# Hidden rows of four groups in one bank, an unrolled edge stage, and the pair adds dealt out anew

## The reference, cut to what matters

```python
s = hs[idx_j]; v = hv[idx_j]                 # rows of the edge's far node, 32 and 32 x 3
ys = Yr_ij[:, 0]; yv = Yr_ij[:, 1:4]         # edge_attr_4
h = ssp(f_ij @ W1 + b1)                      # f_ij: 20 features; ssp = softplus - log 2; h: 32
Wij = (h @ W2 + b2) * rcut_ij[:, None]       # 32 x 6, of which four columns reach the output
edge = concat(s*ys*W0, (v.yv)/sqrt(3)*W1, s*yv*W2, v*ys*W3, ...)
agg = segment_sum(edge, idx_i, num_segments=N)
```

## Time and profile before

| | |
|---|---|
| median of 3 runs | 3580.43 us (3575.29 to 3588.78) |
| the profiled execution | 3578.82 us, its span 3577.0 us |
| busy over the span | PE 74%, PEld 60%, DVE 57%, ACT 37%, POOL 35% |
| granted TensorE clock, mean | 0.882 of full |
| `edges` | 87 to 661 us |
| `experts_down`, `splines`, `experts_up` | 885 to 1300 us |

### The profile page before, as it was taken

One profiled execution on the slowest core, in us unless ns is written; L12 is line 12 of the kernel. 1 busy time (PEld: TensorE's weight loads), 2 busy tenths in 40 slices (PEclk: granted clock), 3 DMA queues, 4 the chain that ended last, 5 costly groups with the idle time before them and its releaser, 6 DMA issues. The chain is left out here.

```text
span 3577.0 us, 43276 instructions
## 1 busy us (share of the span) xinstructions
PE 2652.7 (74%) x13387; PEld 2157.2 (60%) x13387; DVE 2048.1 (57%) x3774; ACT 1323.0 (37%) x2287; POOL 1259.1 (35%) x1067
## 2 busy tenths in 40 slices
PE   2789999501740831499988899888997889973998
PEld 2567777401630200478866788677886778852897
DVE  1788888573225125546754476545775457742762
ACT  1545444200100322336643366433653346530431
POOL 0888888567435320012221123211232012312430
PEclk9999999755975975699999999999999999996999
DMA  6211112262875875221022110221102211124100
GB/s 203 43 36 38 38 35 38 54 176 12 256 243 182 275 208 146 86 58 34 25 86 84 44 43 24 86 75 44 43 27 87 72 43 43 33 79 114 45 27 29
DMA packets 217533, 296.37 MB, mean 83 GB/s; under 512 B 100956, under 2 KB 125346, under 8 KB 212899
## 3 DMA queue, kind: packets, MB, share of 16 engines
q1 hardware_dynamic: 113600, 231.09, 21.4%
q0 software_dynamic: 91008, 49.50, 6.4%
q10 hardware_dynamic: 12768, 13.77, 1.1%
HBM read 226.26 MB, written 67.45 MB: 82 GB/s over the span
## 5 line engine op out<-in xcount | busy, mean ns | idle before, releaser
L2134 POOL TENSOR_SCALAR prob<-prob,rden,linked 125x1250 f32<-125x1250 f32 x160 | 223.9, 1399 | 967.9 <-DVE rden L2101 967.9
L2052 ACT CAST prob_high<-ps 125x375 fp32r<-125x375 f32 (+1 forms) x480 | 231.4, 504 | 266.7 <-PE ps L2014 262.6
L2093 DVE CUSTOM_DVE_ANT_0 prob<-ps,mask 125x1250 f32<-125x1250 f32 x160 | 233.1, 1457 | 132.2 <-PE ps L1990 118.2
L2106 DVE TENSOR_TENSOR prob_low<-ps,prob_high 125x375 fp32r<-125x375 f32 (+1 forms) x480 | 269.8, 585 | 46.7 <-ACT prob_high L2052 46.7
L2003 PE MATMUL ps<-ident,prob 125*125 125x125 f32 x1600 | 252.3, 273 | 17.3 <-POOL prob L2134 10.6
L554 PE MATMUL ps<-onehot,mhi 125*128 125x512 f32 (+1 forms) x960 | 258.6, 379 | 1.9 <-DVE onehot L500 1.9
L333 POOL DMA_INDIRECT Hg<-h_rows,idx x160 | 231.5, 1447 | 74.0 <-POOL idx L328 36.4
L2003 PEld LDWEIGHTS ps<-ident,prob 125*125 125x125 f32 x1600 | 232.4, 187 | 29.7 <-POOL prob L2134 22.9
L554 PE MATMUL ps<-onehot,mlo 125*128 125x512 f32 (+1 forms) x960 | 247.8, 368 | 0.0
L2044 ACT ACTIVATE prob<-prob,top 125x1250 f32<-125x1250 f32 x160 | 214.6, 1341 | 48.5 <-DVE top L2093 39.9
L1631 POOL TENSOR_TENSOR g_row<-g_row,bvo 125x512 f32<-125x512 f32 x80 | 104.1, 1301 | 354.1 <-DMA g_row<-g_d 352.1
(11 more groups left out here) (355 smaller groups left out, 6380.7 us busy)
## 6 DMA issues: line engine op xcount, KB each, us to landing
mask<-mask_d SPq DMA_DIRECT2D x40, 546.9 KB
wd<-L_ffn_Wd SPq DMA_DIRECT2D x84, 256.0 KB, 4.2
wu<-L_ffn_Wu SPq DMA_DIRECT2D x84, 256.0 KB, 4.0
g_row<-g_d SPq DMA_DIRECT2D x80, 250.0 KB
g_d<-g_row SPq DMA_DIRECT2D x70, 250.0 KB
sg_wd<-L_ffn_Wd SPq DMA_DIRECT2D x16, 1024.0 KB, 6.7
pairs<-zeros SPq DMA_DIRECT2D x18, 625.0 KB
y_slots<-u_y ACTq DMA_DIRECT2D x84, 128.0 KB, 3.7
```

The lines of the kernel that those rows point to most:

```text
L2052: s.copy(M.pt[0][:, n % 3, 0:w], T.ps[0:P, 3 + n % 4, 0:w]).then_inc(high, 1)
L2093: v.tensor_tensor_reduce(M.prob[:, r, :], S(u)[0:P, 0:N], M.mask[:, it % MASKS, :], 1.0, 3.0e38, ALU.add, ALU.min, M.top[:, r:r + 1]).then ...
L2106: v.tensor_tensor(M.pt[1][:, n % 3, 0:w], T.ps[0:P, 3 + n % 4, 0:w], M.pt[0][:, n % 3, 0:w].bitcast(F32), ALU.subtract).then_inc(low, 1)
L2134: nc.gpsimd.tensor_scalar(M.prob[:, r, :], M.prob[:, r, :], M.rden[:, r:r + 1], T.linked[:, it:it + 1], ALU.mult, ALU.mult).then_inc(norme ...
```

## The change

- **Hidden rows of four groups in one bank.** W1 lies four times in `w1`, each time in the columns of another quarter of 128, with zeros around it. `hidden` of four groups adds into one bank, so that each group's 32 rows stand in their own partitions. Abs, Relu, Exp, Ln and `act_sum` run once for four groups, over 128 partitions. `turn` and `hidden` run up to eight groups ahead (LOOK).
- **Weights.** The bias comes by a matmul of its own (`one33` with `b2`, 512 columns) in front of the four of `weigh`, into bank 5. `edge_attr_4` is multiplied by the edge weight once at the start, so `wr` goes, and the message products read bank 5 directly; `w_free` comes at the end of the products.
- **Copies.** `turn` reads the features and the fetches read the indices where they lie; GpSimd's copies go.
- **Unrolled.** All loops of the stage are written out, addresses are constants.
- **Banks.** The six chunks of the sums take banks 0 to 4; the two short ones share bank 4, which a matmul of zeros opens.
- **Order.** `mlo` comes ahead of the counts; three waits for VectorE's own results stand at new places. All four one-hot tiles of a group stay on VectorE.
- **Pair adds.** 60 run in the edge stage, 1.5 a group. The rest: 14 in `node_update`, 20 in `expert_norm`, 16 in `route`, 6 in `experts_down`, 20 in `splines` (two behind each tile), 24 in `experts_up` (one behind every third block), where the last wait now stands. The GpSimd loop of `experts_up` is written out too.

```diff
+SG, LOOK = 4, 8
+EARLY_ADDS = 60
@@ input_projection, SP
-                    sp.dma_start(E.w1[:], A["L0_gnn_W1"]).then_inc(w2_in, 16)
-                    sp.dma_start(E.b1[:], A["L0_gnn_b1"]...).then_inc(w2_in, 16)
-                    sp.dma_start(w2raw[0:FF, :], A["L0_gnn_W2"]).then_inc(w2_in, 16)
-                    sp.dma_start(w2raw[FF:FF + 1, :], A["L0_gnn_b2"]...).then_inc(w2_in, 16)
+                    sp.wait_ge(cleared, 2)
+                    for q in range(SG):
+                        r = slice(q * FF, (q + 1) * FF)
+                        sp.dma_start(E.w1[:, q, r], A["L0_gnn_W1"]).then_inc(w2_in, 16)
+                        sp.dma_start(E.b1[r, :], A["L0_gnn_b1"]...).then_inc(w2_in, 16)
+                        sp.dma_start(w2raw[r, :], A["L0_gnn_W2"]).then_inc(w2_in, 16)
+                    for r in (0, 32):
+                        sp.dma_start(b2raw[r:r + 1, :], A["L0_gnn_b2"]...).then_inc(w2_in, 16)
@@ input_projection, VectorE (and six small instructions that split the bias in two rows, E.b2)
+                    nc.vector.tensor_tensor(E.a4[:], E.a4[:], E.rw[:].unsqueeze(2).broadcast_to([P, ET, 4]), ALU.mult)
@@ edges, GpSimd
+                    for g in range(NG):
+                        if g + 2 < NG:
+                            fetch(g + 2)
+                        more = EARLY_ADDS * (g + 1) // NG
+                        pool.wait_ge(idx_ready, more // EG + 1)
+                        pair_adds(pool, nc, T, pairs, n, more)
+                        n = more
@@ edges, ScalarE
+                    for g in range(SG):
+                        features(g)
+                    bend(0)
+                    softplus(0)
+                    for g in range(SG, LOOK - 1):
+                        features(g)
...
@@ edges, VectorE
+                        if g >= 1:
                             hot(g - 1, 1)
-
+                        dve.wait_ge(hg_in[u], (g // 2 + 1) * EG * 16)
+                        step(v.tensor_tensor(q3[:], V, yv, ALU.mult))
                         dve.wait_ge(w_made, g + 1)
-                        step(v.tensor_tensor(wr[:]..., T.ps[0:P, 6, :]..., sc(rw, 128), ALU.mult))
-                        settle()
-                        v.sem_inc(w_free, 1)
+                        step(v.tensor_tensor(u02[:], W[:, :, 0:3:2, :], S.broadcast_to([P, EG, 2, FF]), ALU.mult))
+                        step(v.tensor_tensor(v3[:], W[:, :, 3:4, :].broadcast_to([P, EG, 3, FF]), V, ALU.mult))
...
+                        step(v.scalar_tensor_tensor(M[:, :, 1, :], qs[:], 1.0 / math.sqrt(3.0), W[:, :, 1, :], ALU.mult, ALU.mult))
+                        settle()
+                        v.sem_inc(w_free, 1)
+                        v.sem_inc(msg_ready, 1)
+                        if g >= 1:
                             hot(g - 1, 3)
...
+                    act_sum(0)
+                    for g in range(NG):
+                        messages(g)
+                        hot(g, 0)
+                        q, r = divmod(g + 2, SG)
+                        if r == 0 and SG * q < NG:
+                            act_sum(q)
@@ edges, TensorE
+                        nc.tensor.matmul(T.ps[:, 7, 0:EG * P], E.w1[:, r, :], f20T[:, g % 2, :], start=r == 0,
+                                         stop=r == SG - 1).then_inc(h_made, 1)
...
+                        nc.tensor.matmul(T.ps[0:P, 5, :], E.one33[:], E.b2[:]..., start=True, stop=False)
                         for j in range(EG):
+                            ins = nc.tensor.matmul(T.ps[0:P, 5, j * 128:(j + 1) * 128], hT[rows, q % 2, j * P:(j + 1) * P],
+                                                   E.w2[rows, :, :]..., start=False, stop=j == EG - 1)
...
+                    for g in range(LOOK):
+                        turn(g)
+                        if g >= 1:
+                            hidden(g - 1)
+                    weigh(0)
...
-LATE = ((0, 14), (14, 48), (48, 64), (64, 68), (68, NG // 2 * EG))
+LATE = (EARLY_ADDS, EARLY_ADDS + 14, EARLY_ADDS + 34, EARLY_ADDS + 50, EARLY_ADDS + 56, EARLY_ADDS + 76, ET)
@@ splines, GpSimd
-                    late_adds(pool, nc, T, pairs, 4)
                     for t in range(NT):
...
+                        late_adds(pool, nc, T, pairs, 4, t, NT)
                     for s in t_out:
                         pool.wait_ge(s, 16 * NT // 2)
-                    for s in T.pair_added:
-                        pool.wait_ge(s, ET * 8)
@@ experts_up, GpSimd
+                    n = LATE[5]
+                    for b in range(NB):
+                        if b >= DEEP:
+                            pool.wait_ge(turned, b + 1)
+                        nc.gpsimd.dma_start(hb[:, b % DEEP, :], s_slots[b * BS:(b + 1) * BS, :]).then_inc(h_in[b % DEEP], 16)
+                        if b % 3 == 2 and n < ET:
+                            pair_adds(pool, nc, T, pairs, n, n + 1)
+                            n += 1
+                    for s in T.pair_added:
+                        pool.wait_ge(s, ET * 8)
```

More of the change, by code:

```diff
@@ L361, in ahead @@
-                    def ahead(i, more):
-                        if more:
-                            features(2 * i + 2, 0)
-                            fetch(2 * i + 2, 0)
-                        count(i)
-                        if more:
-                            features(2 * i + 3, 1)
-                            fetch(2 * i + 3, 1)
-                            counted(i)
-                    ahead(0, True)
-                    with pool.Fori(1, NG // 2 - 1) as i:
-                        ahead(i, True)
@@ L415, in _ @@
-                    high(NG - 1, 1)
+                    for g in range(SG, LOOK - 1):
+                        features(g)
+                    for g in range(NG):
+                        if g + LOOK - 1 < NG:
+                            features(g + LOOK - 1)
+                        q, r = divmod(g + LOOK - 2, SG)
+                        ends = r == SG - 1 and g + LOOK - 2 < NG
+                        if ends:
+                            bend(q)
+                        high(g)
+                        if ends:
+                            softplus(q)
@@ L485, in messages @@
+                        step(v.tensor_reduce(E.late_cnt[:, tiles(g)], same[:], AX.X, ALU.add))
                         settle()
```

386 lines of the change are left out of this document (162 added, 224 removed).

## The result

The changed kernel takes 3531.7 us (median of 4 runs, 3527.3 to 3536.8), the kernel before 3579.2 in the same comparison: ratio 0.9858, 95% interval 0.9843 to 0.9873. The prediction was 3530. The profiled execution's span is 3525.6 us, 51.4 less than before. The kernels were compared on several chips, on which the kernel before took 3562 to 3587 us, so runs are compared by their ratio to it, and by stages.

What follows compares the result with a forecast made beforehand. VectorE was taken to set the edge stage's pace, 13.88 us a group, TensorE's work 1.73 shorter. 0.5 - 39 (edge stage) - 20.7 + 5 - 5 + 10 = -49 us from 3578.8 gave about 3530; 8-in-10 range 3496 to 3561.

Steps and rivals of the forecast that it cites:

- First stage: Before the edge stage: 14 more small transfers on SP delay the zeroing, mostly hidden; +0.5 us, +5 if none is.
- Filling: Start of the edge stage: eight groups turned, seven multiplied before the first weigh; first scatter near 125 us, +12 (+9 to +15).
- The period: Edge stage, time per group: 12.5 us instead of 13.88, ends 12.2 and 13.0; both engines at 12.15 to 12.6.
- Rival 1: Edge stage: TensorE becomes the bound at a lowered clock of 0.93, period 13.0, total 3549 us; chance 0.12.
- the gap in front of hidden: Edge stage, TensorE: the gap before the hidden matmuls was to go, saving 0.23 us a group.
- the 0.45 between the quiet and the average group: Edge stage, VectorE: the average group's 0.45 us above a quiet one, part of it to go with GpSimd's lighter work.
- The last group: End of the edge stage: 16 scatter matmuls at 0.583 us each, 9.3 us.
- Normalisation: Normalisation for the experts: 20 pair adds instead of 34, the store of z late next; -20.7 us (-33 to -15).
- Down projection: Ahead of the first pick: 6 pair adds instead of 4; +5 us, 0 if later loads catch up, +6 at worst.
- Splines: Spline stage: 12 adds in one piece become two behind each of ten tiles; -5 us, between -15 and +10.
- Up projection: Up projection: 24 adds, one in three blocks, slow GpSimd's row loads; +10 us, between 0 and +20.
- Rival 4: Unrolled edge stage: TensorE's instruction supply holds groups up, making it slower; 3610 us at 2 us a group, chance 0.05.

Runs made afterwards that it cites:

- no_bias: The changed kernel without the matmul that adds b2 ahead of each weigh; 3530.1 us, ratio 0.9835.
- dve_more: The changed kernel with one more VectorE reduction of the same size (early into a spare tile) in each group; 3560.5 us, ratio 0.9924.
- fill: The changed kernel with TensorE's start of the edge stage reordered, the first weigh ahead of the last three groups' turns and hidden layers; 3528.6 us, ratio 0.9854.
- opt_c: The changed kernel with reordered start, adds dealt anew, and two one-hot tiles a group ahead of VectorE's waits for its own results; 3475.7 us, ratio 0.9760.
- old_adds: The changed kernel with the pair adds spread as in the kernel before, 80 of them in the edge stage; 3548.6 us, ratio 0.9895.
- only_adds: The kernel before with only its late pair adds dealt out anew, 20 instead of 34 in the normalisation; 3562.9 us, ratio 0.9941.
- spl10: The changed kernel with one pair add a spline tile instead of two, and 70 instead of 60 in the edge stage; 3513.6 us, ratio 0.9811.

## Why the prediction was right, point by point
- **First stage, +0.5.** +1.2 (first turn at 89.13 instead of 87.95). With the same code it came at 91.33 in no_bias and 93.75 in dve_more, so the 1.2 is within what executions differ by.
- **Filling, +12.** +14.8 more, 16.0 in all. The first scatter was forecast near 125 and came at 129.09. Of these 4 us, 2.6 are the first turn, which the working began at 86.5 (1.2 of them are the first stage's); about 1.1 the turns and hidden layers, of which the latter take 2.03 us instead of 1.84; 0.7 the bias matmul ahead of the first weigh, which the working left out; 0.5 were regained between the weigh and the scatter. `fill` shows that 5.8 us of the 16.0 were only the order.
- **The period, 12.5 us.** (615.83 - 129.09) / 39 = 12.48 from first scatter to the start of the last group; 12.56 for a group with turn and hidden layer. TensorE sets it: a group follows by 12.15 us without the bias matmul, and still by 12.56 when VectorE gets 0.75 us more of slack (opt_c, 30.7 / 32 - 0.21). The margin is small: with 0.6 more on VectorE the period is 12.98 and VectorE's, and without the bias matmul VectorE is level. I had written that both engines lie at 12.15 to 12.6, and had not said which; VectorE's chain is at 12.35. Rival 1, TensorE as the bound, came true by half: it bounds, but at clock 1.00 and not 0.93. The term that was mis-sized is TensorE's: 12.15 + 0.24 - 0.23 = 12.16 was forecast, and 12.56 came, since the bias matmul costs 0.41 us a group and not 0.24, and nothing was gained at the gap in front of hidden (without the bias matmul the group takes the 12.15 of before). On VectorE one term was not in the list: the one-hot tiles got 0.14 us longer each. Of the 0.45 between the quiet and the average group of before, part of which the working gave to GpSimd's work, some 0.3 went with the lowered clock. So 12.5 was hit with one engine 0.4 us too fast in the working and the other, at 12.6 for 12.35, too slow: the number is in part luck.
- **The last group, 9.3 us.** 11.0. Ahead of it TensorE waits 2.03 us for a one-hot tile, and then runs at half its rate until about 620:

```profile
615.83 0.80 PE L510 MATMUL ps<-onehot,mhi 125*128 125x512 f32 x3 [2.03 <-DVE onehot L401]
...
617.29 1.27 PE L510 MATMUL ps<-onehot,mhi 125*128 125x512 f32 x3
```
```profile
615.00:620.00 5.00, 4.17 (x14) 3.49 (x15) 3.02 (x4) 0.00 (x0) 0.00 (x0) 0.67 0.00 0
```

The granted clock is 0.67 there. The stage's end moved by -34.0 instead of 0.5 - 39 = -38.5: 3.6 from the start, 1.7 here, 0.8 the other way from the period.
- **Normalisation, -20.7.** -24.7 with the node stage; old_adds and only_adds (163.0 and 136.4) show that it is the adds alone. The mechanism was that of the prediction, the store of z is late next. The working let the stage end with its last add at 817.8; it ended at 822.1, 4.3 later, and now ends 1.2 behind the landing of the store, which is 3.1 of the 4 us missed.
- **Down projection, +5.** +6.9 up to the first pick. With 4 adds this stretch takes 72.3 to 74.6 us in six kernels, mean 73.5, with 6 adds 79.7 to 81.4 in seven, mean 80.3: 6.8 us for the two adds, above the +6 that was the worst case. Behind the first pick the down projection takes 135.5 to 147.0 us with the same code, and that -3.6 fell on the changed kernel's execution is luck.
- **Splines, -5.** -0.2. The mechanism held: 8.2 us a tile for seven tiles and then 6.1 were forecast, 8.35 for seven, 7.60 and 6.13 came, 2.6 us more in all. The first store came 1.1 us later than the working had it (38.3 us behind the first row fetch instead of 37.2), and the stage closes 10.3 us behind the last store instead of 8.3, with two adds in between. So what breaking up the piece gained, the second add of a tile took back; spl10 shows its cost: 18 us.
- **Up projection, +10.** +7.4. Over the runs the stage takes 141.6 to 147.4 us with 24 adds, 137.7 to 140.9 with 14, 135.0 and 136.1 with none: about 0.3 us an add, where 0.42 was forecast.
- **Rival 4, instruction supply.** TensorE has no idle time at all before any instruction of a whole unrolled group. The Trainium skill (Runtime: NRT & Kernel Launch, Instruction fetch mechanics) holds that fetching in sequence is hidden; this trace agrees.

The sum, -49 against -51.4 in the traces, held because errors cancelled. The edge stage's end (4.5 us) and the splines (4.8) were too hopeful. The normalisation (4.0), route and down projection (1.7, from +3.3 for +5) and the up projection (2.6) were too cautious, and the stages behind, which I had left out, took 3.2 less. That the total is this close is luck; that each large term has its sign and its cause is not.

What stays open: why VectorE's group took 12.19 us in no_bias, 0.16 less than its chain in the changed kernel; why kd, 4 elements wide, has a length of 0.55 us in most runs and 0.23 in dve_more (at 126.23 us of the changed kernel the next instruction starts 0.13 behind it, so the length cost nothing there); and the spread of the down projection between executions.

## What to carry to other kernels
Idle time of an engine was slack here only where it waited for another engine. VectorE was idle for 8%, four fifths of it at waits for its own results, and 0.6 us more work cost 0.42 us a group; moving independent work ahead of such waits (opt_c) brought the slack that the busy share had promised. A short wait of TensorE could cost more than itself: behind waits of 1.3 to 2.0 us the granted clock of the next 5 us was often 0.53 to 0.77, though not always, so look at the matmuls behind a gap too. Test a bound from both sides, by shortening one engine and lengthening the other, and read the pitch in the middle of the stage, since the ends of it can hide the answer in the total. And small background jobs on a queue are priced by the place: the same pair add cost nothing in the edge stage (495.7 to 499.2 us with 0, 60 or 80 of them), 0.3 us in the up projection, 1.8 us as the second of a spline tile, 2.3 in the node stage, 3.4 ahead of the first pick, and in the normalisation nothing until GpSimd's queue outlasted the store of z.

## What the runs showed of the hardware
At the start of the edge stage scatter matmuls ran at half their rate well into steady work, while the profile's row gave a granted clock of 1.00. In no_bias TensorE works almost without a gap from 130.28 on, and reaches the full rate at about 143.3:

```profile
130.00:140.00 10.00, 9.71 (x25) 6.55 (x26) 7.46 (x16) 2.87 (x5) 8.31 (x6) 1.00 0.22 48
```

In the changed kernel the same happens at about 131.9, 2.8 us behind the first scatter:

```profile
130.27 1.27 PE L510 MATMUL ps<-onehot,mlo 125*128 125x512 f32 x3
...
132.69 0.74 PE L510 MATMUL ps<-onehot,mlo 125*128 125x512 f32 x3
```

So at the start of this stage the pitch of equal instructions (from start to start) tells the rate, and the clock column does not. Inside the stage the two agree: 0.67 in 615 to 620 us of the changed kernel, where three matmuls again start up to 1.07 us apart. The moment of the rise differs by 11 us between kernels that do almost the same work, one execution each.
